# A fused two-layer transformer: when the query and key weights of the first layer are transposed, and in what order the first loads are issued

## The chip, the cores and the metric

The kernel runs on one core of a Trainium2 chip, in one launch. The metric is the device time of the execution in microseconds (us), the median of several runs.

## The reference, cut to what matters

Tokens are x of shape (8, 256, 128). Four residual blocks follow: attention A, a mixture of experts, attention B, and the same mixture of experts. The change touches the start of attention A alone:

```python
x = x + _L0_attn_a_ref(_layernorm(x), w_qkv, w_out, rel_bias)   # 16 heads of 64, all 256 keys
...
qkv = x @ w_qkv.T                                # w_qkv: (3072, 128)
qkv = qkv.reshape(b, t, dh, 3, h).transpose(3, 0, 4, 1, 2)
scores = einsum('bhid,bhjd->bhij', q, k) * scale + bias[h, i, j]
out = softmax(scores) @ v;  out @ w_out.T
```

`w_qkv` is stored with its rows as outputs, so its 24 blocks of 128 by 128 (8 for queries, 8 for keys, 8 for values) have to be transposed on the chip before they can be used as stationary weights. The bias of a head, rel_bias[j - i + 255], comes as a table T of 16 heads by 256 by 128 rows.

## The kernel before, in words

**Units and steps.** A unit u is a pair of heads of one batch element b: 8 units for each of 8 batch elements, so 64 units (NU) in a layer. The program of each engine is written out by hand as a loop over steps s. In step s, TensorE (PE) computes queries and keys of unit s (`QK(s)`, L566) into PSUM bank 0; ScalarE (ACT) copies them to SBUF (`T(s)`, L912). In each odd step PE makes the scores of two units, `S(s - 1)` and `S(s)` (L596), in banks 1, 2 and 3, 7. VectorE (DVE) adds the bias and finds the row minimum, in four passes for each unit (`S(u)`, L1228, with L1246). ACT takes the exponential (`expo`, L938, with L948), DVE the reciprocal of the sums (L1257), GpSimd (POOL) multiplies (`weigh`, L350, with L358) and prepares the bias tables of later units (`biases`, L383, with L389). Four and more steps later PE transposes the probabilities (`TR(s - 4)`, L609) and multiplies them with the values (`PV`, L628) into bank 6.

**The start.** Products in fp32r are made in three passes, of a high and a low part of each operand. So each weight panel is transposed by PE into PSUM (`pe_weights(n)`, L499, four transposes), its high part is taken by ACT (`products`, L979, with L870) and its low part by DVE (`products`, L1326, with L1125 or L1127). There are four such panels n: n = 0 and 1 are queries and keys of units 0 to 3, n = 2 and 3 those of units 4 to 7. `QK(0)` needs n = 0 and 1, `QK(4)` needs n = 2 and 3. The values' weights go the same way in eight transposes (`value_weights`, L776, L1031, L1458). The first tokens are normalised by DVE and transposed by PE (`pre_b(0)`, L526).

**What sets the order.** Each engine works strictly through its own list and waits on semaphores: `t_m` counts transposed panels, `a_m` high parts, `v_m` low parts. `begin` (L768, L1027, L1452) is the part ahead of step 0; there PE transposes the first tokens and then all four panels. The loads are issued by two sequencers, SP (`sp_program`, L1610) and ACT (`act_program`, L1099), each of which issues one half of every piece of `w_qkv`:

```python
        for g in range(2):
            for j, w in enumerate((wqn, wkn)):
                sp.dma_start(w[0:64, 4 * g:4 * g + 4, :], wq3[j, :, 8 * g:8 * g + 7:2, :]).then_inc(d_wqk[g], 16)
        sp.dma_start(wvn[0:64, :, :], wq3[2, :, 0::2, :]).then_inc(d_wv, 16)
        sp.dma_start(a_T[:, 0:4, :], t["bias"][:, 0:4, :]).then_inc(d_T[0], 16)
```

In PSUM panels 0, 1 and 2 use banks 0, 1 and 2, and panel 3 uses bank 6. `held` (L471) says what has to be done before a bank is first taken by something else.

Of the kernel before, what the change touches and what calls it, by code (L numbers as in the profile page):

```python
# [145 lines left out]
def build(nc, t):  # L146
# [3 lines left out]
    def sem(name):  # L150
        return ctx.enter_context(nc.semaphore(name))

    def sb(name, shape, dt=F32, scope=None):
        return (scope or ctx).enter_context(nc.sbuf_tensor(name, shape, dt))
# [68 lines left out]
    def at_first(scope, *made):  # L223

        scope.close()
        return made

    base = ExitStack()
    pre = ExitStack()
    wqn, wkn, wvn = at_first(pre, *(sb(n, [128, 8, 128], scope=pre) for n in ("wqn", "wkn", "wvn")))  # L230
    a_ring = [sb(f"ring{i}", [128, 2, 2, 256], scope=base) for i in range(4)]
    between = ExitStack()
    bq, bo = at_first(between, sb("bq", [128, 1024], scope=between), sb("bo", [128, 8, 128], scope=between))
# [24 lines left out]
    base.close()  # L258


    d_wqk, d_wv, d_x, d_won = [sem("d_wqk0"), sem("d_wqk1")], sem("d_wv"), [sem(f"d_x{i}") for i in range(3)], sem("d_won")
    d_T, d_wr, d_ln = [sem(f"d_T{i}") for i in range(3)], sem("d_wr"), sem("d_ln")
    d_empty, d_clear = [sem(f"d_empty{st}") for st in range(2)], sem("d_clear")
    d_w, d_bq, d_bu, d_bkd, d_bo = sem("d_w"), sem("d_bq"), sem("d_bu"), sem("d_bkd"), sem("d_bo")
# [203 lines left out]
                steps[1](s - OFF)  # L468


    turn, held = [], {0: None, 1: (v_m, 2), 2: (v_m, 3), 3: None, 7: None}  # L471

    def claim(bank, done, n):

# [18 lines left out]
    def tr(out, src):  # L493
        return pe.transpose(out, src, ident[:, :])  # L494

    def m_bank(n):
        return ps[6] if n == 3 else ps[n]

    def pe_weights(n):  # L499

        g, j = divmod(n, 2)
        for c in range(4):
            i = tr(m_bank(n)[:, 128 * c:128 * c + 128], (wqn, wkn)[j][:, 4 * g + c, :])
        i.then_inc(t_m, 1)

    def h_bank(n):
# [13 lines left out]
    def pe_steps(st):  # L520
# [246 lines left out]

        def begin():  # L768
            pe.wait_ge(p_set, k_id)
            pre_b(0)  # L770
            for n in range(4):
                if n % 2 == 0:
                    pe.wait_ge(d_wqk[n // 2], 64)
                pe_weights(n)

        def value_weights():  # L776
            pe.wait_ge(d_wv, 32)
# [5 lines left out]
        def step(s):  # L783
            n = s - F0
            turn[:] = (2, 1) if s == NU else (7, 3) if s < 0 or s > NU else (3, 7, 1, 2) if s % 2 else (1, 2, 3, 7)
            if 0 <= s < NU:
                QK(s)
            if st == 0 and s == 0:
                value_weights()
            for v in VALUES[st].get(s, ()):  # L790
                values(*v)
            if (b := pre_at(s, "b", st)) is not None:
                pre_b(b)
            if st and (b := pre_at(s, "c", st)) is not None:
                pre_c(b)
                if b == 0:
                    first_queries()
            if (b := at(s, 13)) is not None and b < NB - 1:
                out_2(b)
            if s < NU:  # L800
                after(s)
            if 4 <= s < NU + 4:
                TR(s - 4)
            if post_at(s, "b") == NB - 2:
                post_b(NB - 2)
            if s == max(LAST):
                out_last(*LAST[s])
            if n in AT_ONCE:
                if n == F_EACH:
                    Y(n - 2)  # L810
                XT(GROUP_OF[n])
                if n == F_EACH:
                    Y(n - 1)
            if n == NF - 1 and st:
                Y(n - 2)
            if 0 < n < NF:
                H(n)
            if (b := at(s, 12)) is not None and b < NB - 1:
                out(b)
            if s % 2 and 1 <= s < NU:  # L820
                S(s - 1)
                S(s)
            if s % 2 and 5 <= s < NU + 4:
                PV(s - 5)
                PV(s - 4)
            if n == 0:
                XT(0)
            if s in LAST and s < max(LAST):
                out_last(*LAST[s])
            if n == 0:  # L830
                H(0)
            if s == LAST_POST["b"]:
                post_b(NB - 1)
            if n == F_MORE - 1:
                Y(n - 2)
                Y(n - 1)
                Y(n)
            elif 2 <= n < NF + 2 and n not in (*AT_ONCE, F_MORE, F_MORE + 1) and not (st and n == NF - 1):
                Y(n - 2)
            for g in range(1, NG):  # L840
                if n == xt_at(g, st) and GROUPS[g][0] not in AT_ONCE:
                    XT(g)
            if s >= NU:
                after(s)
# [34 lines left out]
    def act_steps(st):  # L879
# [145 lines left out]
            act.activation(f_sub[:, 0:m, :], f_sub[:, 0:m, :], ACT.Exp).then_inc(a_ge, 1)  # L1025

        def begin():  # L1027
            pre_b(0)
            products(0, 1, 2)

        def value_weights():  # L1031
            for g in range(2):
# [3 lines left out]
        def step(s):  # L1036
            n = s - F0
            if s % 2 == 0 and 6 <= s <= NU:
                keep(s - 6)
            if 0 <= s < NU:  # L1040
                T(s)
            if st == 0 and s == 1:
                value_weights()
                products(3)
            if s % 2 and 3 <= s < NU:
                if st and (b := pre_at(s, "c", st)) is not None:
                    pre_c(b)
                after(s)
                expo(s - 3, (1,))
            for v in VALUES[st].get(s, ()):  # L1050
                values(*v)
            if (b := pre_at(s, "b", st)) is not None:
                pre_b(b)
            if not (s % 2 and 3 <= s < NU):
                if st and (b := pre_at(s, "c", st)) is not None:
                    pre_c(b)
                if s < NU:
                    after(s)
            if 4 <= s < NU + 4:
                TR(s - 4)  # L1060
            if 2 <= s < NU + 2:
                expo(s - 2, (0, 1) if s % 2 or s == NU else (0,))
            if n == 0:
                keep(NU - 4)
                XT(0)
            if (b := at(s, 12)) is not None and b < NB - 1:
                out(b)
            if n == F_EACH:
                for m in AT_ONCE:
                    XT(GROUP_OF[m])  # L1070
            if s == LAST_POST["b"]:
                post_b(NB - 1)
            if st == 0 and n <= 11:
                next_weights(n)
            if 0 <= n < NF:
                relu(n)
            if s == LAST_KEEP:
                keep(NU - 2)
            for g in range(1, NG):
                if n == xt_at(g, st) and GROUPS[g][0] not in AT_ONCE:  # L1080
                    XT(g)
            if s >= NU:
                after(s)
            if st == 0 and n > 11:
                next_weights(n)
# [11 lines left out]
        return begin, step  # L1097

    def act_program():  # L1099
        for g in range(2):  # L1100
            for j, w in enumerate((wqn, wkn)):
                act.dma_start(w[64:128, 4 * g:4 * g + 4, :], wq3[j, :, 8 * g + 1:8 * g + 8:2, :]).then_inc(d_wqk[g], 16)
        act.dma_start(wvn[64:128, :, :], wq3[2, :, 1::2, :]).then_inc(d_wv, 16)
        begin, steps = zip(*(act_steps(st) for st in range(2)))
        begin[0]()
        for s in range(OFF + STEPS):
            if s < STEPS:
                steps[0](s)
            if s >= OFF + min(PRE_0.values()):
                steps[1](s - OFF)  # L1110
# [84 lines left out]
    def dve_steps(st):  # L1195
# [256 lines left out]
        def begin():  # L1452
            pre_a(0)
            pre_a2(0)
            pre_b(0)
            products(0, 1, 2)

        def value_weights():  # L1458
            for g in range(2):
# [3 lines left out]
        def step(s):  # L1463
# [4 lines left out]
                start_rows()  # L1468
            if st == 0 and s == 1:
                value_weights()  # L1470
                products(3)
            if s % 2 == 0 and 6 <= s < NU:
                keep(s - 6)
# [31 lines left out]
                pre_a2(b)  # L1505
            if s % 2 and 1 <= s < NU:
                S(s - 1)
                if (b := pre_at(s, "a2", st)) == 1:
                    pre_a2(b)
                if (b := pre_at(s, "a", st)) == 1:  # L1510
                    pre_a(b)
                if s in (NU - 3, NU - 1):
                    weigh(s - 2)
                if s == NU - 1:
                    TR(NU - 4)
                    keep(NU - 6)
                    TR(NU - 3)
                    index(4)
                S(s)
# [89 lines left out]

    def sp_program():  # L1610
        sp.dma_start(x[:, 0:2, :], xv[:, 0:2, :]).then_inc(d_x[0], 16)
        for g in range(2):
            for j, w in enumerate((wqn, wkn)):
                sp.dma_start(w[0:64, 4 * g:4 * g + 4, :], wq3[j, :, 8 * g:8 * g + 7:2, :]).then_inc(d_wqk[g], 16)
        sp.dma_start(wvn[0:64, :, :], wq3[2, :, 0::2, :]).then_inc(d_wv, 16)
        sp.dma_start(a_T[:, 0:4, :], t["bias"][:, 0:4, :]).then_inc(d_T[0], 16)
        sp.dma_start(x[:, 2:4, :], xv[:, 2:4, :]).then_inc(d_x[1], 16)
        sp.dma_start(a_T[:, 4:8, :], t["bias"][:, 4:8, :]).then_inc(d_T[1], 16)
        sp.dma_start(won[:, :], t["w_out_a"]).then_inc(d_won, 16)
# [85 lines left out]
```

## Time and profile before

| | |
|---|---|
| median of 3 runs | 665.16 us (664.17 to 667.16) |
| the profiled execution | 665.05 us |
| its span, first to last instruction | 663.4 us |
| PE busy | 644.6 us, 97% of the span |
| ACT busy | 533.4 us, 80% |
| DVE busy | 475.5 us, 72% |
| POOL busy | 353.6 us, 53% |

The profile is one execution. Busy time is the union of an engine's instructions; a matmul is shown with its latency, so neighbouring ones overlap. A wait is put down to the engine or transfer that came last.

### The profile page before, as it was taken

To read this page: it belongs to the slowest core of one execution; us is meant where nothing else is said; L and a number is where in the kernel's file an instruction comes from. 1 tells how busy PE (TensorE), PEld (TensorE's weight loads), DVE (VectorE), ACT (ScalarE), POOL (GpSimd) and SP (SyncE) were. 2 spreads that over 40 slices of the span, in tenths; PEclk is the share of its full clock that TensorE was granted. 3 is DMA by queue.
4 is the path that set the end of the run, shared out by engine and by line. 5 is a ranking of instruction groups with operands and counts; after the bars stand their busy time and mean duration, and the time that the engine had idled before them with its cause. 6 is when DMAs were issued, how large, how long until landed. Compare 5 with 4: busy or idle time off the path is not lost. (4 is left out here: it accounts for less than half of the span.)

```text
span 663.4 us, 17842 instructions
## 1 busy us (share of the span) xinstructions
PE 644.6 (97%) x5406; PEld 544.2 (82%) x5406; DVE 475.5 (72%) x2147; ACT 533.4 (80%) x1776; POOL 353.6 (53%) x669
## 2 busy tenths in 40 slices
PE   6999999999999999999999999999999999999997
PEld 5778888888888788878997788888888888888997
DVE  4866767777786767988755767687868777898833
ACT  4997888788888879785765989898989898986664
POOL 4654545575546644732116545464757575472737
PEclk9999999999999999999999999999999999999999
DMA  9999989999993000035421000000000000013140
GB/s 272 279 296 293 290 210 312 292 280 285 293 286 95 18 1 1 33 98 167 133 58 45 17 1 1 2 3 9 17 14 9 14 25 2 2 34 101 52 128 20
DMA packets 86844, 74.48 MB, mean 112 GB/s; under 512 B 8001, under 2 KB 83399, under 8 KB 86496
## 3 DMA queue, kind: packets, MB, share of 16 engines
q1 hardware_dynamic: 82288, 66.24, 36.3%
q0 software_dynamic: 2848, 6.33, 2.9%
q10 hardware_dynamic: 1616, 0.79, 0.5%
q8 instruction: 45, 0.74, 0.5%
q14 instruction: 47, 0.39, 0.2%
HBM read 19.93 MB, written 54.00 MB: 111 GB/s over the span
## 5 line engine op out<-in xcount | busy, mean ns | idle before, releaser
L358 POOL TENSOR_SCALAR ring<-ring,rs 128x256 f32<-128x256 f32 (+1 forms) x500 | 218.1, 453 | 206.7 <-DVE rs L1257 206.1
L948 ACT ACTIVATE ring<-ring,mn 128x256 f32<-128x256 f32 (+1 forms) x512 | 243.2, 487 | 1.6 <-DVE mn L1246 1.6
L494 PE MATMUL ps<-ident,ring 128*128 128x128 f32 x896 | 121.1, 275 | 2.7 <-POOL ring L358 1.3
L605 PE MATMUL ps<-qk 64*128 64x256 f32 (+1 forms) x1024 | 115.2, 363 | 0.9 <-DVE mn L1246 0.6
L642 PE MATMUL ps<-pt,v 128*64 128x256 f32 (+1 forms) x1024 | 111.4, 359 | 0.2
L494 PEld LDWEIGHTS ps<-ident,ring 128*128 128x128 f32 x896 | 102.2, 143 | 9.2 <-POOL ring L358 2.4
L948 ACT ACTIVATION_READ_ACCUMULATOR ring<-ring,mn 128x1 f32 x512 | 103.8, 203 | 0.0
L642 PEld LDWEIGHTS ps<-pt,v 128*64 128x64 f32 x1024 | 65.5, 136 | 44.3 <-issue 13.7
L605 PEld LDWEIGHTS ps<-qk 64*128 64x128 f32 x1024 | 82.6, 186 | 18.8 <-issue 10.0
L916 ACT COPY qk<-ps 128x512 f32<-128x512 f32 x128 | 74.7, 584 | 23.7 <-PE ps L491 22.1
L1246 DVE CUSTOM_DVE_ANT_0 ring<-ps,cm 128x128 f32<-128x128 f32 (+1 forms) x256 | 73.8, 350 | 3.5 <-PE ps L605 3.5
L1275 DVE COPY pt<-ps 128x512 f32<-128x512 f32 x64 | 44.1, 690 | 35.3 <-PE ps L494 35.3
L489 PE MATMUL ps<-xth,wqkh 128*128 128x256 f32 x192 | 64.8, 338 | 0.0
L997 ACT ACTIVATE f_ht<-ps,f_w 128x128 f32<-128x128 f32 x136 | 38.4, 377 | 22.6 <-PE ps L747 22.6
L1246 DVE CUSTOM_DVE_ANT_0 ring<-ps,T 128x256 f32<-128x256 f32 x136 | 55.5, 417 | 0.0
L491 PE MATMUL ps<-xtl,wqkh 128*128 128x256 f32 x192 | 53.8, 280 | 0.0
L490 PE MATMUL ps<-xth,wqkl 128*128 128x256 f32 x192 | 53.7, 280 | 0.0
L763 PE MATMUL ps<-w,f_ht 128*128 (+1 forms) x400 | 52.3, 277 | 0.4 <-ACT f_ht L997 0.4
L870 ACT ACTIVATE oh<-ps 128x512 fp32r<-128x512 f32 x64 | 38.3, 598 | 17.4 <-PE ps L642 17.3
L489 PEld LDWEIGHTS ps<-xth,wqkh 128*128 128x128 f32 x192 | 36.2, 189 | 18.6 <-issue 17.5
L1246 DVE CUSTOM_DVE_ANT_1 ring<-ps,T 128x256 f32<-128x256 f32 x120 | 50.0, 417 | 0.2 <-PE ps L605 0.2
L763 PEld LDWEIGHTS ps<-w,f_ht 128*128 128x128 f32 x400 | 48.1, 192 | 1.6 <-issue 1.4
(212 smaller groups left out, 1335.0 us busy)
## 6 DMA issues: line engine op xcount, KB each, us to landing
xs_scratch<-f_ys SPq DMA_DIRECT2D x16, 2064.0 KB, 23.5
yr_scratch<-f_ys SPq DMA_DIRECT2D x8, 1024.0 KB, 10.1
f_xs<-xs_scratch SPq DMA_DIRECT2D x50, 129.0 KB, 2.4
w<-in_W SPq DMA_DIRECT2D x16, 256.0 KB, 5.9
xs_scratch<-f_ys SPq DMA_DIRECT2D x2, 1677.0 KB, 21.4
yr_scratch<-f_ys SPq DMA_DIRECT2D x25, 64.0 KB, 1.5
T<-in_bias SPq DMA_DIRECT2D x2, 512.0 KB, 7.5
T<-in_bias SPq DMA_DIRECT2D x1, 1024.0 KB, 10.2
```

Of the source, the lines that this page charges most:

```text
L358: i = pool.tensor_scalar(ring[:, hh, it, 0:w], ring[:, hh, it, 0:w], rs[:, q], 1.0, ALU.mult, ALU.mult)
L489: pe.matmul(out, ah, bh, start=first, stop=False)
L490: pe.matmul(out, al, bh, start=False, stop=False)
L491: return pe.matmul(out, ah, bl, start=False, stop=last)
L494: return pe.transpose(out, src, ident[:, :])
L605: i = pe.matmul(PS[u % 2][hh][:, 256 * it:256 * it + w], qk[rows, 128 * it:128 * it + 128], qk[rows, 256:256 + w], start=True, stop=True)
L642: i = pe.matmul(PO[64 * hh:64 * hh + 64, col + lo:col + 256], a_v[b % 2][:, jt, 128 * c + 64 * hh:128 * c + 64 * hh + 64], a_pt[(U0 + u) % ...
L763: i = pe.matmul(y_bank(n)[:, 0:128], f_ht[n % 3][:, 128 * f:128 * f + 128], w2[:, bass.ds(e * 4 + f, 1), :].rearrange("p a n -> p (a n)"), ...
L916: act.copy(a_qk[(U0 + u) % 2][:, :], PT_[:, :]).then_inc(a_t, 1)
L948: i = act.activation(ring[:, hh, it, 0:w], ring[:, hh, it, 0:w], ACT.Exp, bias=mn[:, q], scale=-1.0, accum_out=sm[:, q])
L1246: i = dve.tensor_tensor_reduce(ring[:, hh, it, 0:w], bank[:, 256 * it:256 * it + w], table(st, 2 * c + hh, it), 1.0, BIG, ALU.add, ALU.min ...
L1275: i = dve.tensor_copy(pt[:, 1, :], PP[1][:, :])
```

## The change

The panels are kept by halves of units rather than by queries and keys: `wqk0` holds panels 0 and 1, `wqk1` panels 2 and 3, and each panel has a semaphore of its own for its load. Panel 0 is transposed and split ahead of the first tokens, panel 1 behind them. Panels 2 and 3 leave `begin`: PE transposes them at the end of steps 1 and 2, both into bank 6, so that panel 3 waits until DVE has read panel 2 (`v_m` of 3). ACT takes their high parts in steps 2 and 3 behind `T(s)`, DVE their low parts in step 1 between the passes of `S(0)` and `S(1)`, and in step 3 ahead of `weigh(0)`. Among the loads, the first quarter of the table T now goes ahead of SP's half of the values' weights, and both halves of panels 2 and 3 go behind the values' weights.

```diff
--- before.py
+++ after.py
@@ -227,7 +227,9 @@
 
     base = ExitStack()
     pre = ExitStack()
-    wqn, wkn, wvn = at_first(pre, *(sb(n, [128, 8, 128], scope=pre) for n in ("wqn", "wkn", "wvn")))
+
+
+    wqk0, wvn, _, wqk1 = at_first(pre, *(sb(n, [128, 8, 128], scope=pre) for n in ("wqk0", "wvn", "between", "wqk1")))
     a_ring = [sb(f"ring{i}", [128, 2, 2, 256], scope=base) for i in range(4)]
     between = ExitStack()
     bq, bo = at_first(between, sb("bq", [128, 1024], scope=between), sb("bo", [128, 8, 128], scope=between))
@@ -258,7 +260,7 @@
     base.close()
 
 
-    d_wqk, d_wv, d_x, d_won = [sem("d_wqk0"), sem("d_wqk1")], sem("d_wv"), [sem(f"d_x{i}") for i in range(3)], sem("d_won")
+    d_wqk, d_wv, d_x, d_won = [sem(f"d_wqk{i}") for i in range(4)], sem("d_wv"), [sem(f"d_x{i}") for i in range(3)], sem("d_won")
     d_T, d_wr, d_ln = [sem(f"d_T{i}") for i in range(3)], sem("d_wr"), sem("d_ln")
     d_empty, d_clear = [sem(f"d_empty{st}") for st in range(2)], sem("d_clear")
     d_w, d_bq, d_bu, d_bkd, d_bo = sem("d_w"), sem("d_bq"), sem("d_bu"), sem("d_bkd"), sem("d_bo")
@@ -468,7 +470,7 @@
                 steps[1](s - OFF)
 
 
-    turn, held = [], {0: None, 1: (v_m, 2), 2: (v_m, 3), 3: None, 7: None}
+    turn, held = [], {0: None, 1: (v_m, 2), 2: None, 3: None, 7: None}
 
     def claim(bank, done, n):
 
@@ -494,13 +496,16 @@
         return pe.transpose(out, src, ident[:, :])
 
     def m_bank(n):
-        return ps[6] if n == 3 else ps[n]
+        return ps[6] if n >= 2 else ps[n]
 
     def pe_weights(n):
 
         g, j = divmod(n, 2)
+        pe.wait_ge(d_wqk[n], 32)
+        if n == 3:
+            pe.wait_ge(v_m, 3)
         for c in range(4):
-            i = tr(m_bank(n)[:, 128 * c:128 * c + 128], (wqn, wkn)[j][:, 4 * g + c, :])
+            i = tr(m_bank(n)[:, 128 * c:128 * c + 128], (wqk0, wqk1)[g][:, 4 * j + c, :])
         i.then_inc(t_m, 1)
 
     def h_bank(n):
@@ -767,11 +772,9 @@
 
         def begin():
             pe.wait_ge(p_set, k_id)
+            pe_weights(0)
             pre_b(0)
-            for n in range(4):
-                if n % 2 == 0:
-                    pe.wait_ge(d_wqk[n // 2], 64)
-                pe_weights(n)
+            pe_weights(1)
 
         def value_weights():
             pe.wait_ge(d_wv, 32)
@@ -825,6 +828,8 @@
                 PV(s - 4)
             if n == 0:
                 XT(0)
+            if st == 0 and s in (1, 2):
+                pe_weights(s + 1)
             if s in LAST and s < max(LAST):
                 out_last(*LAST[s])
             if n == 0:
@@ -1025,8 +1030,9 @@
             act.activation(f_sub[:, 0:m, :], f_sub[:, 0:m, :], ACT.Exp).then_inc(a_ge, 1)
 
         def begin():
+            products(0)
             pre_b(0)
-            products(0, 1, 2)
+            products(1)
 
         def value_weights():
             for g in range(2):
@@ -1041,7 +1047,8 @@
                 T(s)
             if st == 0 and s == 1:
                 value_weights()
-                products(3)
+            if st == 0 and s in (2, 3):
+                products(s)
             if s % 2 and 3 <= s < NU:
                 if st and (b := pre_at(s, "c", st)) is not None:
                     pre_c(b)
@@ -1097,10 +1104,11 @@
         return begin, step
 
     def act_program():
-        for g in range(2):
-            for j, w in enumerate((wqn, wkn)):
-                act.dma_start(w[64:128, 4 * g:4 * g + 4, :], wq3[j, :, 8 * g + 1:8 * g + 8:2, :]).then_inc(d_wqk[g], 16)
+        for j in range(2):
+            act.dma_start(wqk0[64:128, 4 * j:4 * j + 4, :], wq3[j, :, 1:8:2, :]).then_inc(d_wqk[j], 16)
         act.dma_start(wvn[64:128, :, :], wq3[2, :, 1::2, :]).then_inc(d_wv, 16)
+        for j in range(2):
+            act.dma_start(wqk1[64:128, 4 * j:4 * j + 4, :], wq3[j, :, 9:16:2, :]).then_inc(d_wqk[2 + j], 16)
         begin, steps = zip(*(act_steps(st) for st in range(2)))
         begin[0]()
         for s in range(OFF + STEPS):
@@ -1452,8 +1460,9 @@
         def begin():
             pre_a(0)
             pre_a2(0)
+            products(0)
             pre_b(0)
-            products(0, 1, 2)
+            products(1)
 
         def value_weights():
             for g in range(2):
@@ -1468,6 +1477,7 @@
                 start_rows()
             if st == 0 and s == 1:
                 value_weights()
+            if st == 0 and s == 3:
                 products(3)
             if s % 2 == 0 and 6 <= s < NU:
                 keep(s - 6)
@@ -1505,6 +1515,8 @@
                 pre_a2(b)
             if s % 2 and 1 <= s < NU:
                 S(s - 1)
+                if st == 0 and s == 1:
+                    products(2)
                 if (b := pre_at(s, "a2", st)) == 1:
                     pre_a2(b)
                 if (b := pre_at(s, "a", st)) == 1:
@@ -1609,11 +1621,12 @@
 
     def sp_program():
         sp.dma_start(x[:, 0:2, :], xv[:, 0:2, :]).then_inc(d_x[0], 16)
-        for g in range(2):
-            for j, w in enumerate((wqn, wkn)):
-                sp.dma_start(w[0:64, 4 * g:4 * g + 4, :], wq3[j, :, 8 * g:8 * g + 7:2, :]).then_inc(d_wqk[g], 16)
+        for j in range(2):
+            sp.dma_start(wqk0[0:64, 4 * j:4 * j + 4, :], wq3[j, :, 0:7:2, :]).then_inc(d_wqk[j], 16)
+        sp.dma_start(a_T[:, 0:4, :], t["bias"][:, 0:4, :]).then_inc(d_T[0], 16)
         sp.dma_start(wvn[0:64, :, :], wq3[2, :, 0::2, :]).then_inc(d_wv, 16)
-        sp.dma_start(a_T[:, 0:4, :], t["bias"][:, 0:4, :]).then_inc(d_T[0], 16)
+        for j in range(2):
+            sp.dma_start(wqk1[0:64, 4 * j:4 * j + 4, :], wq3[j, :, 8:15:2, :]).then_inc(d_wqk[2 + j], 16)
         sp.dma_start(x[:, 2:4, :], xv[:, 2:4, :]).then_inc(d_x[1], 16)
         sp.dma_start(a_T[:, 4:8, :], t["bias"][:, 4:8, :]).then_inc(d_T[1], 16)
         sp.dma_start(won[:, :], t["w_out_a"]).then_inc(d_won, 16)
```

On PE this is the start before (ps: PSUM; xh: the first tokens; wqn, wkn: weights of queries, keys; wvn: of values):

```order
L494 MATMUL ps<-ident,xh 128x128 x2
L494 MATMUL ps<-ident,wqn 128x128 x4
L494 MATMUL ps<-ident,wkn 128x128 x4
L494 MATMUL ps<-ident,wqn 128x128 x4
L494 MATMUL ps<-ident,wkn 128x128 x4
L489 MATMUL ps<-xth,wqkh 128x256
```

and this the start now (wqk is wqk0), with its waits:

```order
L496 MATMUL ps<-ident,wqk 128x128 [waits barrier_Pool_Activation_PE_DVE_SP_release,d_wqk0,p_set]
L496 MATMUL ps<-ident,wqk 128x128 x3
L496 MATMUL ps<-ident,xh 128x128 [waits v_xh]
L496 MATMUL ps<-ident,xh 128x128
L496 MATMUL ps<-ident,wqk 128x128 [waits d_wqk1]
L496 MATMUL ps<-ident,wqk 128x128 x3
L491 MATMUL ps<-xth,wqkh 128x256 [waits v_x,a_m,a_x,v_m]
```

Eight transposes are gone from in front of the first product of `QK(0)`. They stand further down on PE now: these rows run from the scores of step 1 (L610) over `QK(2)` to panel 3, behind which `QK(3)` follows.

```order
L610 MATMUL ps<-qk 128x256 x3
L496 MATMUL ps<-ident,wqk 128x128 [waits d_wqk2]
L496 MATMUL ps<-ident,wqk 128x128 x3
L491 MATMUL ps<-xth,wqkh 128x256 [waits a_t]
L492 MATMUL ps<-xth,wqkl 128x256
L493 MATMUL ps<-xtl,wqkh 128x256
L491 MATMUL ps<-xth,wqkh 128x256
L492 MATMUL ps<-xth,wqkl 128x256
L493 MATMUL ps<-xtl,wqkh 128x256
L491 MATMUL ps<-wvh,xth 128x512 [waits a_wv,v_wv,v_x,a_x]
L492 MATMUL ps<-wvh,xtl 128x512
L493 MATMUL ps<-wvl,xth 128x512
L496 MATMUL ps<-ident,wqk 128x128 [waits v_m,d_wqk3]
```

Panel 2 waits for its load alone, panel 3 for DVE (`v_m`) and its load, and all of PE's list stands behind that wait. On DVE, before, panel 3's low part (wqkl) stood ahead of the first pass of the scores:

```order
L1125 TENSOR_TENSOR wvl<-ps,wvh 128x512 [waits a_wv,v_c]
L1125 TENSOR_TENSOR wvl<-ps,wvh 128x512 [waits a_wv]
L1125 TENSOR_TENSOR wqkl<-ps,wqkh 128x512 [waits a_m]
L1246 ISA ring,mn<-ps,T 128x256 [waits t_s,p_set]
```

and now the last rows of `S(0)` are followed by panel 2, which waits for ACT (`a_m`):

```order
L1254 ISA ring,mn<-ps,T 128x256
L1254 ISA mn 128x1
L1135 SCALAR_TENSOR_TENSOR wqkl<-ps,wqkh 128x512 [waits a_m]
L1140 BN_STATS stats<-row 128x6 [waits d_x1]
```

So one low part went from ahead of `S(0)` to behind it, and panel 3's stands behind `S(1)` (not shown).

## Rows read from the trace of the kernel before

**Rows 1.** Busy time in stretches: start and end, length, engines, granted clock, DMA.
```profile
40.00:280.00 240.00, 240.00 (x1947) 196.12 (x1946) 175.02 (x758) 201.48 (x620) 132.58 (x256) 1.00 0.73 198
```

**Rows 2.** Timeline, PE ahead of step 0: start, length, operation, count, idle before.
```profile
6.22 1.09 PE L494 MATMUL ps<-ident,wqn 128*128 128x128 f32 x4
...
8.48 1.11 PE L494 MATMUL ps<-ident,wqn 128*128 128x128 f32 x4 [0.32 <-DMA wkn<-in_w_qkv]
...
10.10 0.56 PE L489 MATMUL ps<-xth,wqkh 128*128 128x256 f32 x1
```

**Rows 3.** Timeline, loads issued by ACT and SP: start, length.
```profile
1.32 0.72 SPq L1614 DMA_DIRECT2D wqn<-in_w_qkv  x1
...
2.09 0.60 SPq L1614 DMA_DIRECT2D wkn<-in_w_qkv  x1
...
4.05 0.62 SPq L1615 DMA_DIRECT2D wvn<-in_w_qkv  x1
```

**Rows 4.** The same loads in the view of DMA issues: KB, us to landing.
```profile
wqn<-in_w_qkv SPq DMA_DIRECT2D x1, 128.0 KB, 3.3
wkn<-in_w_qkv SPq DMA_DIRECT2D x1, 128.0 KB, 4.1
wvn<-in_w_qkv SPq DMA_DIRECT2D x1, 256.0 KB, 6.8
```

**Rows 5.** Busy time in stretches, the last number being GB/s moved.
```profile
6.20:10.85 4.65, 4.33 (x22) 3.93 (x21) 2.40 (x4) 2.17 (x4) 3.15 (x14) 1.00 1.05 260
10.85:12.00 1.15, 1.15 (x13) 1.11 (x12) 0.18 (x2) 0.59 (x1) 0.00 (x0) 1.00 1.12 388
```

**Rows 6.** Timeline, PE from the values' weights on to step 3.
```profile
11.15 1.04 PE L494 MATMUL ps<-ident,wvn 128*128 128x128 f32 x8
...
12.88 2.00 PE L605 MATMUL ps<-qk 64*128 64x256 f32 x16
...
14.81 0.39 PE L489 MATMUL ps<-xth,wqkh 128*128 128x256 f32 x1
...
16.46 0.39 PE L489 MATMUL ps<-xth,wqkh 128*128 128x256 f32 x1
...
19.84 1.13 PE L605 MATMUL ps<-qk 64*128 64x256 f32 x8 [0.65 <-DVE mn L1246]
```

**Rows 7.** Timeline, DVE in steps 0 to 3.
```profile
12.10 0.17 DVE L1225 COPY cT<-T 128x4 f32<-128x4 f32 x1 [1.07 <-DMA T<-in_bias]
...
14.18 1.29 DVE L1125 TENSOR_TENSOR wvl<-ps,wvh 128x512 fp32r<-128x512 f32 x2 [0.65 <-ACT wvh L870]
...
15.98 0.41 DVE L1246 CUSTOM_DVE_ANT_1 ring<-ps,T 128x256 f32<-128x256 f32 x1
...
18.23 0.42 DVE L1246 CUSTOM_DVE_ANT_1 ring<-ps,T 128x256 f32<-128x256 f32 x1
...
19.65 0.18 DVE L1257 RECIPROCAL rs<-sm 128x4 f32<-128x4 f32 x1
```

**Rows 8.** Timeline, ACT in steps 1 to 3.
```profile
13.47 1.09 ACT L870 ACTIVATE wvh<-ps 128x512 fp32r<-128x512 f32 x2
...
15.82 0.59 ACT L916 COPY qk<-ps 128x512 f32<-128x512 f32 x1 [0.76 <-PE ps L491]
...
18.06 0.57 ACT L916 COPY qk<-ps 128x512 f32<-128x512 f32 x1
```

**Rows 9.** Timeline, POOL in steps 3 and 4.
```profile
19.93 1.90 POOL L358 TENSOR_SCALAR ring<-ring,rs 128x256 f32<-128x256 f32 x4 [0.81 <-DVE rs L1257]
...
22.05 1.89 POOL L389 TENSOR_TENSOR T<-cT,T 128x1024 f32<-128x1024 f32 x1
...
23.92 1.84 POOL L358 TENSOR_SCALAR ring<-ring,rs 128x256 f32<-128x256 f32 x4
```

**Rows 10.** Timeline, PE in step 5.
```profile
25.91 0.60 PE L494 MATMUL ps<-ident,ring 128*128 128x128 f32 x4
...
27.25 2.00 PE L605 MATMUL ps<-qk 64*128 64x256 f32 x16
```

## Prediction, made before the changed kernel was run

> **What bounds the kernel now.** I first read the page's busy times: PE is at work 97% of the span, so what counts is when PE gets its work, not how long the others take. Then the busy time in stretches, the whole span cut up. From 40 to 280 us PE is busy in every microsecond, while ACT has 38 us to spare of 240, DVE 65 and POOL more [rows 1]. From this follows the rule of the whole estimate: **a microsecond that PE loses or gains in the first steps stays to the end of the first attention**, for no idle time of PE is left there that could swallow it. Nor do I see a place behind it that waits for something with a time of its own: the transfers behind the layers start from results, so they move too. All that is left is to find out by how much PE's first uninterrupted work moves. For that I read the timeline of 0 to 30 us engine by engine, and the view of DMA issues for the landings.
>
> **The start before.** PE transposes the four panels from 6.22 on and stands for the second pair's load up to 8.48; `QK(0)` follows at 10.10 [rows 2]. The values' weights were asked for by SP at 4.05 and took 6.8 us, so they landed at 10.85 [rows 3, 4], and PE took them at 11.15 behind `QK(0)` [rows 6]. ACT splits them at 13.47 [rows 8], DVE at 14.18, and DVE's first pass of the scores starts at 15.98 [rows 7]. The reader should see that the chain is one of handing over, PE to ACT to DVE, where nobody is full.
>
> **The change, step by step.**
>
> *Panel 0 ahead of the tokens.* Its second half landed at 1.32 + 3.3 = 4.6 [rows 3, 4], and four transposes take 1.09 [rows 2]: done by 5.7, in PE's idle time, since PE has no other work than the two small transposes of the tokens before 6.22. No cost. Panel 1 landed at 2.09 + 4.1 = 6.2 [rows 3, 4]; it now stands where panel 0 stood. High and low part take about 0.6 and 0.7 more, so `QK(0)` can start near 8.7 and not at 10.10: **1.4 us sooner**. This gain can't be kept whole, since PE's next work is the values' weights.
>
> *Values' weights.* Up to 10.85 there had landed 128 KB of tokens, 1024 KB of panels, 512 KB of values' weights and a part of T. Now it is 128 + 512 + 512 KB and 512 KB of T, the same bytes, and in addition between 0 and 256 KB of panels 2 and 3 that ACT's sequencer issues. The pieces of w_qkv moved at 260 GB/s, the stretch in which T took over at 388 [rows 5]: 512 KB at the second rate save 0.7 us, 256 KB at the first cost 1.0. With the part of T that was in already (some 0.3 us) the bounds are 9.9 and 11.2. I take the middle, 10.5, an estimate: PE takes the values' weights at 10.5 for 11.15, **0.65 us sooner**. The Trainium skill, DMA: Bandwidth & Descriptors, section Issuing engines are not separate DMA queues, speaks against more: transfers that different engines issue end up on the same DMA engines and interleave. By that rule ACT's panels run beside SP's values' weights and the upper bound of 11.2 is the likely one, which would make the sum 0.7 us worse. No row of this trace shows the new order, so I leave the middle.
>
> *T sooner.* DVE waited 1.07 us for T up to 12.10 [rows 7], but behind its pass over T it stood again for 0.65 us, until the values' low part could start at 14.18 [rows 7]: the pass was over at 13.53. By itself T sooner gains nothing. It is needed though: with the values' weights 0.65 sooner that low part starts at 13.53, just when T would have been ready.
>
> *DVE's first pass.* Before: 14.18 to 15.98 for three low parts, 0.60 each [rows 7]. Panel 3 is no longer among them. So `S(0)` starts at 15.98 - 0.65 - 0.60 = 14.73 and takes 1.42 (from 18.23 to 19.65, as `S(1)` does [rows 7]), to 16.15. Up to here the change is 1.25 us ahead.
>
> *Panel 2 in step 1.* PE's scores of units 0 and 1 move to 12.23 and take the 1.93 us up to the next work [rows 6]: 14.16. Four transposes at the later speed, half of the eight in 1.04 [rows 6], add 0.52. `QK(2)` starts at 14.68 for 14.81. Its copy `T(2)` follows 1.01 later, as 15.82 does 14.81 [rows 6, 8]: 15.69. ACT's next slot is 0.49 on, and a high part lasts 0.60 (the pair takes 1.09 [rows 8]): ready at 16.8. **DVE, free at 16.15, waits for it**, and gives the low part at 17.45.
>
> *Panel 3 behind it.* Both panels use bank 6, so PE waits for that low part at the end of step 2, and its whole list stands behind this wait: 17.45 plus 0.52 makes `QK(3)` start at 17.97 instead of 16.46 [rows 6], **1.5 us later**. What PE did in that time before, values and `QK(3)`, it did early and without need; so this is not yet the price.
>
> *Who waits for QK(3).* `T(3)` on ACT comes 1.01 behind it, at 18.98 for 18.06 [rows 8], 0.92 later. Behind `T(3)` ACT now has panel 3's high part, another 0.49. The second pair of exponentials of unit 0 stands behind both, 1.4 later, and with it DVE's reciprocal, which I put at 21.0 for 19.65 [rows 7]. POOL waits for that: it weighs unit 0 from 19.93, prepares a bias table from 22.05, weighs unit 1 from 23.92, back to back [rows 9]. All of it moves by about 1.3. The last one ended at 25.76, and PE transposes unit 1 at 25.91 [rows 10], directly on it. **PE is 1.3 us later at its transposes of step 5**, then at the scores of units 4 and 5 (27.25 [rows 10]), and from there on it is full. DVE's panel 3 (0.60) lies in the time in which DVE would wait for the reciprocal anyway.
>
> **The sum.** PE's own work is the same number of transposes. The gain of 1.25 at DVE's first pass is spent by the wait for panel 2, and what remains is +1.3 us: 665.05 + 1.3 = 666.35, say 666.4 us. The profiled execution, 665.05, lies 0.11 below the median of 665.16. Bounds for the terms: 0.6 less or 0.7 more through the landing of the values' weights (9.9 or 11.2), and, if POOL's chain has slack that I don't see, the weaker shift through `S(3)`. That one waited for DVE's passes of unit 1 up to 19.84 [rows 6]; by PE's list (`QK(3)` at 17.97, with the values some 1.4 as between 14.81 and 16.46, then `S(2)`, 1.0) it would start at about 20.3 [rows 6], +0.5. The forecast's own range is 665.5 to 667.1.
>
> **Rivals.**
>
> *The head start survives.* If panel 3's wait holds nobody who matters, or ACT gets panel 2 sooner than I reckon, PE keeps the 0.65 us of the values' weights: 664.4 us. For it: PE stood 0.65 us at 19.84 [rows 6], so the early steps have slack. Against it: the chain from `QK(2)` over ACT and DVE to PE has no slack in my sum, and POOL is back to back [rows 9]. Chance 0.11.
>
> *The values' weights land no sooner, or later.* This is the change not doing what it says for the start: T's 512 KB in SP's queue now stand ahead of them. At worst they land when before all of this and T had landed, at 12.0 (10.85 plus the 1.15 us of [rows 5]). PE then is another 1.5 us behind: 667.9 us. Against it: 512 KB of panels less are in front. Chance 0.11.
>
> *The slow clock lasts longer: the slower side.* The same four transposes take 1.09 us at 6.22 [rows 2] and about 0.52 at 11.15 [rows 6]: the engine goes from the lower level (1.2 GHz) to the higher (2.4) between them, though the column of the granted clock reads 1.00 throughout. Before it rose PE had been busy 4.33 of 4.65 us [rows 5]. Now PE has gaps there: from about 7.3, when panel 1 is done, to 8.7, and again before the values' weights. If the rise comes only after the scores of units 0 and 1, then the values' transposes cost 1.0 more, `QK(1)` 0.7 (as long as from the end of those transposes, 12.19, to 12.88) and the 16 products 2.0 [rows 6]: 3.7 on top of 1.3, 670.1 us. It passes +3.3 us once the lower level lasts into the second half of those products. The Trainium skill, TensorE: Matmul & The Clock Gate, Part 1, gives the reason: the slow state is the default, activity releases it and idling brings it back. By that rule fewer busy microseconds before 10.7 mean a later rise, which this trace doesn't contradict, but PE also starts a microsecond sooner. Chance 0.07.
>
> **How the numbers follow.** Forecast 0.71, the rivals 0.11, 0.11 and 0.07. About 0.5% or 3.3 us is what a measurement of this kernel can tell from no change (its runs alone spread over 3.0 us). The forecast and the first two rivals are all within it. Slower by over 0.5%, that is over 668.5, takes the clock rival, in most of its cases, and the upper end of the late landing: 0.08. Faster by over 0.5%, below 661.8, has no mechanism in these rows, since even the whole 1.4 us of `QK(0)` is less: 0.02. Within: 0.90. The range of 664.2 to 668.4 holds the forecast, the surviving head start and the late landing, and leaves out the slow clock and the outer runs.
>
> **What would show it.** In the changed profile: `QK(0)` near 8.7; the values' transposes between 9.9 and 11.2; DVE's first pass near 14.7; DVE idle some 0.7 us before panel 2's low part; **PE idle before panel 3's transposes up to about 17.4, put down to DVE**; `T(3)` near 19.0, POOL's first weighting near 21.2; the scores of units 4 and 5 at 28.5 for 27.25, and from 40 us on the same list of work at the same distance. I am wrong if those scores start before 27.25, if PE shows idle time between 40 and 280 us, or if the first transposes at the higher speed come later than 14 us.

## The result, and the profile after

| | before | changed |
|---|---|---|
| median, 6 runs each | 665.97 us | 669.99 us |
| ratio | | 1.0063 (95%: 1.0049 to 1.0078) |
| profiled span | 663.4 us | 668.6 us |
| PE's scores of units 4 and 5 start at | 27.25 us | 32.60 us |

The change costs 0.6%. I had forecast no difference, 666.4 us, with a range up to 668.4. The last line of the table is the one to follow through what comes: 5.35 us are lost by then, and the span is 5.2 us longer. The busy time in stretches says the same for the rest, as PE is full there as it was before [rows 1]:

```profile
40.00:280.00 240.00, 240.00 (x1946) 196.05 (x1945) 173.74 (x750) 202.06 (x623) 130.86 (x252) 1.00 0.74 202
```

The timeline of PE's start in the changed kernel (start, length, operation, idle before), to be laid beside [rows 2, 6, 10]:

```profile
9.26 0.55 PE L491 MATMUL ps<-xth,wqkh 128*128 128x256 f32 x1 [1.50 <-DVE wqkl L1133]
...
11.92 1.97 PE L496 MATMUL ps<-ident,wvn 128*128 128x128 f32 x8 [1.05 <-DMA wvn<-in_w_qkv]
...
15.11 3.15 PE L610 MATMUL ps<-qk 64*128 64x256 f32 x16
...
18.19 0.66 PE L496 MATMUL ps<-ident,wqk 128*128 128x128 f32 x4
...
21.55 0.63 PE L496 MATMUL ps<-ident,wqk 128*128 128x128 f32 x4 [1.30 <-DVE wqkl L1135]
...
32.60 2.00 PE L610 MATMUL ps<-qk 64*128 64x256 f32 x16
```

Three things stand in it. PE waits for the values' weights and takes them at 11.92, not at 11.15. Their eight transposes last 1.97 us for 1.04, and the 16 score products 3.15 for 2.00: **PE is at its lower level up to within the scores of step 1**, where before the level had risen by 11.15. It rises near 17.4 us, by an estimate: from 15.11 to the next work at 18.19 are 3.08 us for 1.93 before, so that some 10 of the 16 products took 0.24 us and the rest 0.12. Panel 2 at 18.19 has the first transposes at the higher level. That is the third of the signs of being wrong that I had named, transposes at the higher speed only after 14 us. And panel 3 waits 1.30 us for DVE's low part of panel 2. The view of DMA issues gives the landings (the number at the end is us from the issue, which was at 2.7 for T and 3.4 for the values' weights):

```profile
T<-in_bias SPq DMA_DIRECT2D x1, 512.0 KB, 7.3
wvn<-in_w_qkv SPq DMA_DIRECT2D x1, 256.0 KB, 8.5
```

T landed at 10.0 for 12.0, but the values' weights at 11.9 for 10.85. On ACT and DVE the steps came in the order that was forecast, only later (DVE's first pass of the scores at 17.61 for 14.7). DVE's idle time before panel 2's low part (third row) is the wait for ACT's high part:

```profile
16.40 1.29 DVE L1133 TENSOR_TENSOR wvl<-ps,wvh 128x512 fp32r<-128x512 f32 x2 [4.75 <-ACT wvh L875]
...
17.61 0.42 DVE L1254 CUSTOM_DVE_ANT_1 ring<-ps,T 128x256 f32<-128x256 f32 x1
...
20.71 0.69 DVE L1135 SCALAR_TENSOR_TENSOR wqkl<-ps,wqkh 128x512 fp32r<-128x512 f32 x1 [1.65 <-ACT wqkh L875]
```

### The profile page after: what moved, and what is told of

Its sections match the earlier page's. It is cut to its first block and busy times, and to the rows that moved or that the text cites. A ratio compares the mean times of both kernels' runs of the same rounds, so it can differ in the third digit from the quotient of the medians.

```text
span 668.6 us, 17843 instructions
## 1 busy us (share of the span) xinstructions
PE 646.9 (97%) x5406; PEld 545.8 (82%) x5406; DVE 475.6 (71%) x2147; ACT 533.5 (80%) x1776; POOL 354.6 (53%) x669
## 3 DMA queue, kind: packets, MB, share of 16 engines
HBM read 19.93 MB, written 54.00 MB: 111 GB/s over the span
## 5 line engine op out<-in xcount | busy, mean ns | idle before, releaser
L610 PE MATMUL ps<-qk 64*128 64x256 f32 (+1 forms) x1024 | 116.1, 366 | 0.2 <-ACT qk L921 0.2
L610 PEld LDWEIGHTS ps<-qk 64*128 64x128 f32 x1024 | 83.5, 188 | 18.3 <-issue 8.8
## 6 DMA issues: line engine op xcount, KB each, us to landing
yr_scratch<-f_ys SPq DMA_DIRECT2D x8, 1024.0 KB, 10.7
```

Of the source, the lines that this page charges most:

```text
L610: i = pe.matmul(PS[u % 2][hh][:, 256 * it:256 * it + w], qk[rows, 128 * it:128 * it + 128], qk[rows, 256:256 + w], start=True, stop=True)
```

## The experiments

**How they are read.** The effects are of 1 to 3 us, and one run of this kernel differs from the next by as much. So each is read from its profiled execution, by two times of PE: when it takes the values' weights, and when it starts the scores of units 4 and 5. The distance between them turned out to be fixed by the program and the clock. Where all panels are in `begin` and the clock is up, it is 27.25 - 11.15 = 16.10 us before, and was 16.10 again in e4 and e8. The last column compares each run's timed executions with those of the kernel before that were taken beside it.

| run | values' weights taken | scores of 4, 5 | distance | ratio to before (95%) |
|---|---|---|---|---|
| before | 11.15 | 27.25 | 16.10 | |
| changed | 11.92 | 32.60 | 20.68 | 1.0063 (1.0049 to 1.0078) |
| e1 | 12.93 | 31.03 | 18.10 | 1.0051 (1.0038 to 1.0065) |
| e2 | 11.10 | 31.10 | 20.00 | 1.0058 (1.0041 to 1.0076) |
| e3 | 11.87 | 31.80 | 19.93 | 1.0061 (1.0048 to 1.0074) |
| e4 | 11.51 | 27.61 | 16.10 | 0.9999 (0.9990 to 1.0007) |
| e5 | 10.73 | 28.83 | 18.10 | 1.0033 (1.0021 to 1.0046) |
| e6 | 11.84 | 29.04 | 17.20 | 1.0017 (1.0005 to 1.0029) |
| e7 | 14.12 | 32.96 | 18.84 | 1.0060 (1.0043 to 1.0077) |
| e8 | 12.18 | 28.28 | 16.10 | 1.0007 (0.9993 to 1.0020) |
| e9 | 10.62 | 29.42 | 18.80 | 1.0044 (1.0031 to 1.0056) |
| e10 | 10.78 | 27.92 | 17.14 | 1.0006 (0.9995 to 1.0017) |

**e1, PE kept busy.** The changed kernel with spare transposes in its two gaps:

```diff
             pe_weights(1)
+            keep_busy(6)
...
+        def keep_busy(m):
+            for _ in range(m):
+                tr(ps[6][:, 0:128], ident[:, :])
...
         def value_weights():
+            keep_busy(5)
             pe.wait_ge(d_wv, 32)
```

> The changed kernel, with 6 spare transposes of the identity on PE behind panel 1 and 5 behind QK(0), into bank 6, which nobody reads: they fill PE's idle time before QK(0) and before the values' weights, and change nothing else. Theory (slow clock): idle time kept PE at the lower level up to the scores of step 1; filled, the level rises near 10.7 us as in the kernel before, PE's scores of units 4 and 5 start near 29.9 (27.25 before, 32.60 changed), and the time is some 2.7 us below the changed kernel's, +2.6 us against before (ratio about 1.004). Rival (only the landings and panel 3's wait count): the spare work costs up to 1 us and nothing is gained, scores at 32.6 or later, ratio 1.006 to 1.008.

```profile
7.47 1.49 PE L496 MATMUL ps<-ident 128*128 128x128 f32 x6
...
10.53 0.71 PE L496 MATMUL ps<-ident 128*128 128x128 f32 x5
...
12.93 1.09 PE L496 MATMUL ps<-ident,wvn 128*128 128x128 f32 x8 [1.69 <-DMA wvn<-in_w_qkv]
14.67 2.00 PE L610 MATMUL ps<-qk 64*128 64x256 f32 x16
```

The five spare transposes at 10.53 already go at the higher level, and so do all real ones. The distance falls from 20.68 to 18.10: **the late clock was worth 2.58 us**. Nothing was taken out of the program, work was added. The values' weights landed 1.0 later than in the changed kernel, with the same order of loads, which is why the scores are at 31.03 and not at 29.9 as expected.

**e2, the loads as before,** panels 2 and 3 ahead of the values' weights, T behind them:

> The changed kernel with the loads in the order of before: panels 2 and 3 ahead of the values' weights, T behind them. Theory (landing of the values' weights is a term of its own, about 1.1 us): they land at 10.85 instead of 11.9. If the clock still rises late (17.4), the scores of units 4 and 5 start at 32.1, only 0.5 below the changed kernel, since PE is slow anyway; if PE's shorter gap lets it rise at about 14, near 30.5; if at 10.7, near 28.8. Rival (T asked for sooner is a gain for DVE): 32.6 or later.

The values' weights were taken at 11.10, that is 0.8 sooner. The clock rose during the scores of step 1 as well, but sooner (16 products in 2.44 us), so 1.90 us of it were left in the distance of 20.00. Late landing and late clock are two terms.

**e3, panel 3 in a bank of its own:**

```diff
-        return ps[6] if n >= 2 else ps[n]
+        return ps[{2: 6, 3: 5}.get(n, n)]
...
-        if n == 3:
-            pe.wait_ge(v_m, 3)
...
-                PX = PP[k - 1]
+                PX = ps[(4, 6)[k - 1]]
+                if k == 2:
+                    pe.wait_ge(v_m, 3)
```

> The changed kernel with panel 3 in bank 5 and the first half of the values of the second 128 tokens in bank 6, so that PE's transposes of panel 3 no longer wait for DVE's low part of panel 2 (the values wait for it, behind QK(3)). Theory (the sum of the prediction): that wait is on the path over QK(3), T(3), the exponentials and POOL; T(3) starts 0.85 us sooner and the scores of units 4 and 5 at 31.8 instead of 32.6, the time 0.8 us below the changed kernel's. Rival (PE's hold reaches nobody): scores at 32.6, no difference.

```profile
20.16 0.60 PE L496 MATMUL ps<-ident,wqk 128*128 128x128 f32 x4
```

The wait ahead of panel 3 is gone, and the scores start at 31.80, as expected. The wait for DVE is worth 0.8 us of PE's time here.

**e4, panel 0 ahead of the tokens alone.** Panels 1, 2, 3 follow in `begin`, `products(3)` is in step 1 again, and the loads are in the old order.

> One part of the change alone: panel 0 goes ahead of the first tokens, with semaphores for each panel; panels 2 and 3 stay in begin, and the loads in the order of before. Theory: PE then has no gap longer than before's in the first 11 us, the clock rises as before, QK(0) stands behind panel 3 as before, and the scores of units 4 and 5 start at 27.2, no difference to before within 0.2 us (ratio 1.000). Rival (the new head itself is what cost time, by delaying the tokens' low part): 0.5 us later or more.

The ratio is 0.9999 and the distance 16.10, so this part of the change is free, and it gains nothing either. The scores are 0.4 late of what was expected since the values' weights were (11.51). The clock was up by then, without any spare work: the 12 transposes of three panels keep PE busy by themselves.

**e5 and e6, what is left with the clock and the loads mended.** e5 is e1 with the loads of e2; e6 adds the banks of e3.

> The changed kernel with the loads in the order of before and the spare transposes of e1, so that neither the landing nor the clock differ from before: what is left is the place of panels 2 and 3. Theory: the clock rises near 10.4 us, the values' weights are taken at 10.9, and the scores of units 4 and 5 start at 28.4 to 28.8, 1.2 to 1.6 us behind before (27.25), ratio 1.002. Rival (the clock and the landings were all of it): 27.2, ratio 1.000.

> e5 with panel 3 in bank 5 as in e3, so that it waits for nobody. Theory: 0.8 us of the place of the panels was that wait, the rest is ACT's and DVE's work, which stands ahead of the exponentials and of the reciprocal; scores of units 4 and 5 at 27.6 to 28.0, ratio 1.001. Rival (the wait is all of the place): 27.2, as before.

```profile
17.75 0.63 PE L496 MATMUL ps<-ident,wqk 128*128 128x128 f32 x4 [1.30 <-DVE wqkl L1141]
```

The rival of e5 falls: with nothing wrong in clock or loads, the distance is 18.10, and the kernel is 0.33% slower than before. **The place of panels 2 and 3 costs 2.00 us**, of which e6 gives back 0.90 (17.20). The other 1.10 stand on DVE, ahead of its first reciprocal of the sums (before: 19.65 [rows 7]). These rows are from e6:

```profile
14.86 1.29 DVE L1139 TENSOR_TENSOR wvl<-ps,wvh 128x512 fp32r<-128x512 f32 x2 [0.42 <-ACT wvh L881]
...
18.03 0.69 DVE L1141 SCALAR_TENSOR_TENSOR wqkl<-ps,wqkh 128x512 fp32r<-128x512 f32 x1 [0.50 <-ACT wqkh L881]
...
21.48 0.17 DVE L1271 RECIPROCAL rs<-sm 128x4 f32<-128x4 f32 x1
```

From the values' low part to the reciprocal DVE needs 6.62 us (14.86 to 21.48), and 5.47 before (14.18 to 19.65). In between it takes one low part more (0.60) and stands 0.50 us for ACT's high part of panel 2. And **the scores of units 4 and 5 follow that reciprocal by a fixed time**: 7.60 us before (27.25 - 19.65), 7.60 in the changed kernel (32.60 - 25.00), 7.56 in e6, and between 7.55 and 7.61 in each of the twelve kernels. PE does have more work of its own in the stretch, busy 16.33 us of e6's 17.20 for 15.30 of 16.10 before, since panels 2 and 3 now lie in it; that this work costs time by itself isn't shown.

The clock shows in the timed runs here too: e5 differs from e2 by the spare transposes alone and has 1.0033 for 1.0058 (the intervals just overlap). e6's scores come at 29.04, 1.0 above what was expected, because its values' weights landed at 11.8 (7.7 us after the issue; e5's took 6.6): with the same order of loads the landing differs by a microsecond from run to run.

**e7, T alone moved ahead,** in e4:

```diff
+        sp.dma_start(a_T[:, 0:4, :], t["bias"][:, 0:4, :]).then_inc(d_T[0], 16)
         sp.dma_start(wvn[0:64, :, :], wq3[2, :, 0::2, :]).then_inc(d_wv, 16)
-        sp.dma_start(a_T[:, 0:4, :], t["bias"][:, 0:4, :]).then_inc(d_T[0], 16)
```

> e4 (panel 0 ahead of the tokens, panels 2 and 3 in begin) with one load moved: the first quarter of T goes ahead of SP's half of the values' weights, as in the change. Theory: T lands near 10.9 instead of 12.0 and the values' weights at 11.9 instead of 10.9 to 11.5; the scores of units 4 and 5 start 0.6 to 1.0 us later than in e4 (27.61), at 28.2 to 28.6. Rival (the first panels' halves were what delayed the values' weights): 27.6, no difference to e4.

```profile
14.12 1.97 PE L496 MATMUL ps<-ident,wvn 128*128 128x128 f32 x8 [3.45 <-DMA wvn<-in_w_qkv]
```

The busy time in stretches, with the granted clock ahead of the last two columns:

```profile
9.50:13.00 3.50, 1.17 (x9) 0.97 (x7) 1.32 (x4) 0.59 (x1) 0.83 (x3) 1.00 1.13 236
13.00:16.00 3.00, 1.88 (x9) 1.88 (x10) 0.65 (x1) 0.00 (x0) 0.24 (x2) 0.54 1.04 410
16.00:19.50 3.50, 3.50 (x17) 2.93 (x18) 0.91 (x2) 2.06 (x4) 1.85 (x1) 0.50 1.06 345
```

One load a place further up cost more than expected: the values' weights were taken 2.6 us later than in e4, PE stood for 3.45 us, **and the clock, which had been up, fell back to 0.50 of full speed** and stayed there while PE was busy again. That second blow is worth 18.84 - 16.10 = 2.74 us. The ratio of 1.0060 is that of the whole change, by one line.

**e8, the kernel before with 16 spare transposes ahead of the tokens:**

> The kernel before, with 16 spare transposes of the identity on PE ahead of the first tokens, from 1.8 us on, into bank 6. Theory (idle and busy set the clock): it rises earlier than 10.7, panels 1 to 3 and QK(0) go faster, but the values' weights, landed at 10.85, cap the gain at 0.5 us: scores of units 4 and 5 at 26.8, ratio 0.999 to 1.000, at best the fastest of all. Rival (the level doesn't hang on what PE does): the rise stays at 10.7 and the scores at 27.25.

```profile
1.60 3.67 PE L494 MATMUL ps<-ident 128*128 128x128 f32 x16 [1.60 <-POOL ident L315]
...
6.09 0.66 PE L494 MATMUL ps<-ident,wqn 128*128 128x128 f32 x4
...
9.13 1.12 PE L494 MATMUL ps<-ident,wqn 128*128 128x128 f32 x4 [1.94 <-DMA wkn<-in_w_qkv]
```

The clock did rise sooner, panel 0 takes 0.66 us for 1.09. But PE then stood 1.94 us for the load of panels 2 and 3, and the granted clock of 9 to 10 us reads 0.50 again:

```profile
9.00:10.00 1.00, 0.87 (x4) 0.88 (x5) 0.00 (x0) 0.00 (x0) 0.66 (x5) 0.50 1.20 208
```

Nothing was gained (1.0007, not to be told from no change): work that ends sooner only makes the next gap longer.

**e9, T back behind the values' weights,** the rest of the change as it is:

> The changed kernel with one line moved back: T's first quarter goes behind SP's half of the values' weights, panels 2 and 3 stay behind both. Theory (T's 512 KB ahead is what made the values' weights late): they land before 10.5 us for 11.9, and PE takes them at 10.5 to 10.9, right behind QK(0). From there the place of the panels fixes 18.1 us to the scores of units 4 and 5 (16.1 before), plus 0 to 2.6 for the clock, so they start between 28.6 and 31.5, the ratio is 1.002 to 1.005. Rival (T has no part in it, ACT's panels took the time): 11.9 again, scores at 32.6, ratio 1.006.

```profile
10.62 1.81 PE L496 MATMUL ps<-ident,wvn 128*128 128x128 f32 x8
```

The weights had landed at 10.0 (2.7 + 7.3), and PE takes them at 10.62 without a wait. PE has no gap ahead of them, the clock rose at their end, and only 0.70 us of the late clock is left (18.80 - 18.10). The scores start at 29.42, 3.2 us sooner than in the changed kernel, with one line moved: 1.30 of it is the landing and 1.88 the clock. The ratio falls to 1.0044.

**e10, all three mended:**

> All three mended at once: T behind the values' weights, the spare transposes that fill PE's gaps, and panel 3 in bank 5. Theory: the terms add up: values' weights taken at 10.2 to 10.8, then 17.2 us to the scores of units 4 and 5, which start at 27.4 to 28.0, ratio 1.000 to 1.001, no better than before. Rival (with the late start mended the head start shows): scores ahead of 27.25 and the ratio below 0.999.

The distance is 17.14, for 17.2 expected, and the ratio 1.0006. The terms add up, and what is left of the idea is no better than the kernel before. No version among these is faster than the kernel before.

## Why the prediction was wrong

Of the 5.35 us, the profiled executions give 0.77 to the values' weights being taken late (11.92 for 11.15), 2.58 to the clock (changed against e1) and 2.00 to the place of the panels (e5 against before). They add up because e1 and e5 have the same distance, 18.10, though their values' weights landed 2.2 us apart; 0.90 of the last is the wait of panel 3 for DVE. The terms aren't independent of each other: T's place alone, moved back in e9, gives 3.18 us back, since the later landing also lengthened the gap ahead of the values' weights. The medians differ by 4.0 us and not by 5.35; which of the terms the timed runs had in what size isn't shown.

*Right: the place of the panels, and that the shift stays.* From the values' weights at 10.5 to the scores at 28.5 I had 18.0 us; measured are 18.1 (e1, e5). In e5, where clock and loads are as before, the steps stand as forecast, counted from the values' weights: `T(3)` 8.41 behind them (8.48 forecast), DVE's reciprocal 10.50 (10.5), POOL's first weighting 10.78 (10.7). What stays open is the last link, over POOL. POOL's second weighting ends 0.15 us before PE's transposes of unit 1 in e5 as before (27.34 and 27.49; 25.76 and 25.91), but PE came to these without idle time, and its waits shortly before were for DVE (0.20 at 24.23 and 0.34 at 25.00 in e5). I had read the 25.91 of [rows 10] as a wait for POOL, which it doesn't show. Both chains start from the reciprocal, and no run separates them. No later idle time of PE took any of it back. I had put panel 3's wait at the centre, and it is nearly half of this term, not all.

*Right: panel 0 is free, and the gain at `QK(0)` can't be kept* (e4). The gain itself was 0.84 us (9.26 for 10.10), not 1.4.

*Wrong, the step "Values' weights": 10.5, with bounds of 9.9 and 11.2.* They landed at 11.9 and, in e1, at 12.9. I let T's 512 KB move at the rate of 388 GB/s at which it had moved alone [rows 5]. In the changed kernel T ran beside ACT's pieces of w_qkv, and from 6.20 to 10.85 us the rate was no better than before:

```profile
6.20:10.85 4.65, 3.15 (x14) 2.50 (x12) 2.54 (x6) 1.47 (x3) 3.32 (x15) 1.00 1.10 242
```

So the credit of 0.7 us was not there. The upper bound I had from the count of bytes, when it should have been the 12.0 of the late rival, from landings. That rival had a chance of 0.11, and for the landing it is what came. And ACT's two panels, issued at 3.0 and 3.7 us, landed at 10.3 and 11.8, ahead of SP's weights, as the Trainium skill has it (DMA: Bandwidth & Descriptors, Issuing engines are not separate DMA queues: they interleave on the same engines). I cited that rule, saw that it made the upper bound the likely one, and kept the middle. Here the trace agrees with it. But e9 shows that T's place made the lateness: without it the weights landed at 10.0, sooner than the 10.85 of before, and beside the same two panels.

*Wrong, the clock, which I gave 0.07 as a rival.* The mechanism was described; its price was put at 3.7 us, and 2.58 was measured, since the 16 products cost 1.16 more and not 2.0 (3.08 us to the next work, and 1.92 in e1): the level rose within them and not behind them. Above all the chance was off. That its 670.1 us lies beside the measured 669.99 is in part luck: the price was 1.1 too high, and the late landing, 1.4 us (11.92 for 10.5), was not in it. I set "PE starts a microsecond sooner" against the gaps. It doesn't count against them: PE stood for 1.5 us before `QK(0)` and over a microsecond before the values' weights, and the level rose only within the scores of step 1, near 17.4, where before the values' transposes at 11.15 had it. I should have compared PE's busy time before 10.7 us in the two orders. The eight transposes that the change removes had filled it: with the loads as before and these transposes gone the clock still costs 1.90 us (e2), with them in place nothing (e4), and e1 gets it back by adding idle work. T's place then made it worse (0.70 in e9, 2.58 in the changed kernel). The Trainium skill's page TensorE: Matmul & The Clock Gate, Part 1 (slow is the default, activity releases it, idling brings it back) agrees with e1, and e7 and e8 show the fall.

What also stays open: the timed runs have no trace, so how often the late clock occurs in them isn't known. e1 has the clock mended, yet its ratio of 1.0051 lies within the interval of the changed kernel's 1.0063. Its profiled execution had the latest landing of all with this order, and whether the timed ones had it too can't be seen.

## What to carry to other kernels

Before moving work out of an engine's start-up, ask what the engine does in the time that comes free. Here the gap on TensorE cost 2.58 us, since the clock rose later for everything behind it, and the eight transposes that left had taken PE 1.62 us (8.48 to 10.10 [rows 2]). A load that is asked for sooner pushes back all behind it in its queue; compare who waits last for each. And the idle time in the head of a program was the place for this one-off work: behind it the same transposes and copies cost 2.00 us, as they stood in a chain that passes from engine to engine.

## What the runs showed of the hardware

With a gap of 3.45 us on TensorE (e7) the granted clock fell from 1.00 to 0.50, and with one of 1.94 us at 7.2 us (e8) too, while with the gap of 1.69 us in e1 it did not. In both the fall began while PE still stood (0.63 from 13 to 14 us in e7, 0.88 from 8 to 9 us in e8). The column reads 1.00 from the start of each of these traces up to such a fall, in the changed kernel throughout, though the values' transposes took 1.97 us for 1.04 there. So at a program's start the length of a known instruction tells the level, the column doesn't. And the same 256 KB, with the same loads ahead of them, landed 6.6, 7.0, 7.4 and 7.7 us after their issue in e5, e2, e4 and e6.
